# One queue of transfers moved from SyncE to ScalarE, one mean folded into weights, and a new order on five engines

## What is computed

```python
x = x + _L0_conv_ref(_gn(x), ...)      # masked relu, then a 3x3 convolution
x = x + _L1_conv_ref(_gn(x), ...)      # layer norm and a recurrent layer over 784 tokens

def step(carry, inp):                  # one chunk of 16 tokens, 8 heads of 16 channels
    W1c, b1c = carry
    xq, xk, xv, et = inp
    Z1 = xk @ W1c + b1c
    grad = _ln_l2_bwd(Z1, xv - xk, g, bb)
    Attn1 = jnp.tril(xq @ xk.swapaxes(-1, -2))
    b1_bar = b1c - jnp.tril(et) @ grad
    Z1_bar = xq @ W1c - et * Attn1 @ grad + b1_bar
    last_eta = et[..., -1, :, None]
    W1n = W1c - (last_eta * xk).swapaxes(-1, -2) @ grad
    b1n = b1c - (last_eta * grad).sum(-2, keepdims=True)
    return ((W1n, b1n), xq + _ln(Z1_bar, g, bb, EPS_IN))
...
return _ln(out, post_w, post_b, EPS_IN) @ o_w.T
```

## Time and profile before

| what | value |
|---|---|
| three runs | 2008.76, 2009.25, 2012.17 us |
| profiled execution, its span | 2010.2 us |
| PE busy over the span | 1569.5 us (78%) |
| DVE busy | 1582.3 us (79%) |
| POOL busy | 1317.2 us (66%) |
| ACT busy | 977.5 us (49%) |
| first store of the scan to the last | 576.7 to 2005.4 us |

### The profile page before, as it was taken

One profiled execution on the slowest core, in us unless ns is written; L12 is line 12 of the kernel. 1 busy time (PEld: TensorE's weight loads), 2 busy tenths in 40 slices (PEclk: granted clock), 3 DMA queues, 4 the chain that ended last, 5 costly groups with the idle time before them and its releaser, 6 DMA issues.

```text
span 2010.2 us, 82699 instructions
## 1 busy us (share of the span) xinstructions
PE 1569.5 (78%) x33518; PEld 1214.9 (60%) x33518; DVE 1582.3 (79%) x3818; ACT 977.5 (49%) x2358; POOL 1317.2 (66%) x1479
## 2 busy tenths in 40 slices
PE   1886978914678887888788888878887888888886
PEld 1443544502567676677676766766776766767664
DVE  6989998706687877788878878887888788788774
ACT  2223545443455555555555545555555555555452
POOL 1244535465677777777767777777777777677763
PEclk9998989965666667666656666666666666666655
DMA  6058697962555655556656556666565566566553
GB/s 235 1 30 44 98 98 68 77 159 45 65 70 66 76 71 68 73 67 77 74 65 77 70 69 74 72 71 73 67 77 73 67 77 73 65 76 73 69 68 44
DMA packets 1656796, 148.89 MB, mean 74 GB/s; under 512 B 1636448, under 2 KB 1650016, under 8 KB 1656416
## 3 DMA queue, kind: packets, MB, share of 16 engines
q1 hardware_dynamic: 1396912, 117.90, 49.9%
q10 hardware_dynamic: 259504, 25.70, 10.1%
HBM read 40.71 MB, written 38.54 MB: 39 GB/s over the span
## 4 chain that ended last, share of the span: by engine, by line
SPq 54%; PE 17%; DVE 12%; DMA 7%; issue 6%; POOL 3%; ACT 2%; POOLq 0%; DVEq 0%; ACTq 0%
SPq L486 25%; SPq L519 13%; SPq L479 12%; DMA late<-work 3%; PE p_m L1678 3%; PE p_x L1693 3%; DMA xs_scratch<-work 2%; SPq L438 2%; PE p_j L1557 2%; DVE work L1007 2%; SPq L440 1%; DVE work L1033 1%; PE p_y L1736 1%; PE p_y L1693 1%; PE p_out L1752 1%
## 5 line engine op out<-in xcount | busy, mean ns | idle before, releaser
L1648 PE MATMUL p_kt<-fold,kqk 128*128 128x16 f16 x6272 | 199.4, 174 | 166.9 <-DMA kqk<-work 162.8
L1648 PEld LDWEIGHTS p_kt<-fold,kqk 128*128 128x128 f16 x6272 | 190.6, 104 | 197.9 <-issue 161.3
L808 ACT ACTIVATE work<-p_kt 128x512 f16<-128x512 f32 x196 | 146.9, 750 | 317.8 <-PE p_kt L1648 317.8
L1557 PE MATMUL p_j<-work 128*128 128x392 f16 x864 | 158.5, 345 | 22.2 <-DVE work L1131 20.7
L578 POOL TENSOR_TENSOR work<-work,row 128x256 f32<-128x256 f32 x98 | 96.9, 988 | 113.2 <-DVE work L1437 113.2
L1316 DVE TENSOR_TENSOR work<-work 128x256 f16<-128x256 f32 x196 | 155.2, 842 | 15.4 <-ACT work L795 15.4
L1621 PE MATMUL p_j<-wa,work 128*128 128x512 f16 x196 | 119.4, 609 | 58.4 <-DMA work<-xs_scratch_tail 30.0
L590 POOL TENSOR_TENSOR w<-wst,w 128x256 f16<-128x256 f32 x98 | 75.5, 770 | 127.8 <-ACT w L855 127.8
L1693 PEld LDWEIGHTS p_x<-w,late 128*128 128x128 f16 x4704 | 149.5, 106 | 12.0
L634 POOL TENSOR_TENSOR work<-work,rope_s 128x256 f32<-128x256 f32 x196 | 141.0, 740 | 20.0 <-DVE work L1283 20.0
L645 POOL TENSOR_TENSOR work<-work 128x512 f32<-128x512 f32 x98 | 130.8, 1335 | 30.4 <-DVE work L1307 30.1
(11 more groups left out here) (171 smaller groups left out, 4474.3 us busy)
## 6 DMA issues: line engine op xcount, KB each, us to landing
late<-work SPq DMA_DIRECT2D x1176, 32.0 KB, 2.7
kqk<-work SPq DMA_DIRECT2D x392, 64.0 KB, 4.2
out_y<-work ACTq DMA_DIRECT2D x49, 256.0 KB, 6.4
x_scratch<-late SPq DMA_DIRECT2D x24, 392.0 KB, 11.7
xs_scratch<-work SPq DMA_DIRECT2D x24, 392.0 KB, 6.7
work<-x_scratch ACTq DMA_DIRECT2D x49, 192.0 KB, 3.4
work<-xs_scratch SPq DMA_DIRECT2D x48, 192.0 KB, 3.4
late<-in_x SPq DMA_DIRECT2D x8, 784.0 KB, 9.0
```

What stands on the lines that cost most here:

```text
L808: return act.activation(kqt16[:, o, g:g + GP, :, :, :].rearrange("p g h t a -> p g a (h t)"), p_kt[:, :].rearrange("p (g a n) -> p g a n", ...
L1557: mm = pe.matmul(p_conv[b % 2][h][:, 0:HALF].rearrange("o (i j) -> o i j", j=W), convw16[:, w, t, :], pad[:, b % 2, a, r:r + ROWS, c:c + W ...
L1648: mm = pe.matmul(p_kt[:, at:at + CS], part_of(g + k, h, a), fold16[:, :], start=True, stop=True)
```

## The change

`qt_spread` moves from SyncE's program to ScalarE's, where it stands behind the second `qt_copy` of a chunk. Its eight transfers, their sources, destinations and semaphores stay as they are. `rate_gate` still computes Sigmoid on ScalarE. The mean over channels is taken out of the output weights once (`wo_p` minus its mean over the input channels), so the post norm no longer subtracts the mean: `post_shift` goes, and `post_norm` only scales. That costs one more matmul in `fold_tables` and one more subtraction in `fold_weights`. The order inside `turn` is new on all five engines. Most offsets change by whole turns too; PE runs 53 turns instead of 54, SyncE 51 instead of 53.

```diff
+        def turned_parts(c, o):
+            part = kqt16[:, o, :, :, :, :].rearrange("p g h t a -> p (g h) (t a)")
+            return part, ktqt[c % 2][:, o, :, :, :, :, :].rearrange("p g h b t a -> p (g h) b (t a)")
...
             def turn(k):
-                m_spread(k - 4)
-                kt_spread(k - 3)
-                qt_spread(k - 3)
-                kq_spread(k - 2)
                 xs_next(k)
+                kt_spread(k - 2)
+                kq_spread(k - 1)
+                m_spread(k - 2)
...
             @guard_chunk
+            def qt_spread(c):
+                act.wait_ge(qt_copy_done.sem, qt_copy_done.count(2 * c + 1))
+                if c < 2:
+                    act.wait_ge(s_kt_zero[c], 1)
+                else:
+                    act.wait_ge(o_done.sem, o_done.count(2 * c - 3))
+                part, whole = turned_parts(c, 0)
+                for b in range(GB):
+                    at = slice(b * CS, (b + 1) * CS)
+                    act.dma_start(whole[at, :, b, :], part[at]).then_inc(qt_landed.sem(c), 16)
...
-                act.wait_ge(post_shift_done.sem, post_shift_done.count(s))
+                act.wait_ge(post_inverse_done.sem, post_inverse_done.count(s))
...
-                    last = act.activation(on[:, k * C:(k + 1) * C], oo[:, k * C:(k + 1) * C], ACT.Identity, bias=ostd[:, 2, k:k + 1],
-                                          scale=ostd[:, 1, k:k + 1])
+                    last = act.activation(on[:, k * C:(k + 1) * C], oo[:, k * C:(k + 1) * C], ACT.Copy, scale=ostd[:, 1, k:k + 1])
...
             def turn(k):
+                rate_gate(k - 2)
+                z_square(2 * k - 5)
...
+                folded(dve.tensor_tensor(wo_p[:, :], wo_p[:, :], p_x[1][:, SC:SC + C], ALU.subtract))
...
-            def post_shift(s):
...
-                dve.scalar_tensor_tensor(out=ostd[:, 2, :], in0=omv[:, :, 0], scalar=-1.0, in1=ostd[:, 1, :],
-                                         op0=ALU.mult, op1=ALU.mult).then_inc(post_shift_done.sem, 1)
...
+                pe.matmul(p_x[1][:, SC:SC + C], mean_m, wo_p[:, :], start=True, stop=True).then_inc(s_fold, 1)
```

196 lines of the change are left out of this document (88 added, 108 removed).

## The result

| | before | after |
|---|---|---|
| median on the same chip | 2010.72 us (2008.76 to 2016.13, 6 runs) | 2002.45 us (1999.01 to 2004.82, 6 runs) |
| ratio after/before, 95% interval | | 0.9952 [0.9938, 0.9967] |
| profiled execution's span | 2010.2 us | 1997.1 us |
| one turn, from store to store in the middle of the scan | 30.69 us | 30.59 us |

The change gives half a per cent. Only about 4 us of it come from the turns (44 x 0.1 us); in the profiled executions the first store of the scan also comes 6.3 us earlier, at 570.4 us instead of 576.7. The forecast was 1895 us with a range of 1795 to 1985, so the prediction was wrong: the direction held, the size did not, and the time lies above the range.

The account below looks back on a forecast made before the run. The prediction took SyncE's queue of transfer starts as the bound; afterwards two loops, through the folds and through PE, would give a turn of 28.1 us, 2.6 less over 44 turns: 114 us off, so 1895 us, range 1795 to 1985.

Parts of the forecast that it names:

- What bounds the kernel now: SyncE's queue before the change: it starts transfers all the time, 34 starts at 0.9 us fill a turn of 30.7 us.
- Transfers: SyncE keeps 26 of 34 starts, 23.4 us; the eight moved to ScalarE cost 5.2 us, between 3.4 and 7.06.
- The loop through the folds: From one chunk's last fold through copy, ScalarE's starts, g_high, qk_low and kq_spread to the next chunk's last fold: 28.2 us.
- rival 1: Faster than forecast: PE's work alone bounds, turns of 25.5 to 27 us, 1781 to 1847 us; chance 0.20.
- The loop through PE: PE's steps between folds, 20.9 us, plus 7.0 of folds: 27.9 us, 28.6 in the worst case with the table load.
- The hope of a higher clock: On PE: denser work may hold the higher clock for longer, taking 0.5 to 1 us off its loop.
- The table load's price: In PE's loop: the page's 1.38 us of drain per load would give near 30 us, the trace's rows 28.6.
- Small sizes: DVE 23.6 us and POOL 22.8 stay below the loops; added weight folding at most 1 us; pipeline filling unchanged within 8 us.
- Rival 2: Transfers on the two queues get in each other's way: turns of 29 to 30.5 us, 1935 to 2001 us; chance 0.18.
- Rival 4: Slower: ScalarE held up by its own starts, past 30.7 us a turn from 7.65 us of starts, up to 2067 us; chance 0.06.
- Rival 3: Nothing moves because the transfers themselves set the turn: 30.7 us a turn, 2010 us; chance 0.02.
- What was to show it: Signs if right: stores 28.1 us apart, SyncE waiting at kq_spread, ScalarE's starts 4 to 6 us, folds 7, PE over 0.88.

Follow-up runs that it names:

- e6: The kernel before with only the output weights centred (no post_shift, post_norm only scales): 2016.70 us, ratio 1.0007.
- e10: The changed kernel with seven of turned k's eight transfers on SyncE left out: 1959.72 us, a single run.
- e11: The changed kernel with ScalarE's store and loads exchanged, the store now at the end of the turn: 1989.26 us, ratio 0.9886.
- e1: The changed kernel with only one of turned q's eight transfers started on ScalarE, seven left out: 1939.97 us, a single run.
- e14: The changed kernel with turned q's transfers split four and four between ScalarE and SyncE, Sqrt table loaded behind rate_gate, 64 bytes of tile added: 1896.49 us, ratio 0.9459.
- e15: The changed kernel, eight starts kept on ScalarE, with the Sqrt table loaded behind rate_gate and 64 bytes of tile added: 1956.03 us, ratio 0.9758.

## Why the prediction was wrong

**What bounds the kernel now.** Right. 34 starts filled the turn, and e6 shows it from the other side: with 1.3 us of VectorE's work taken out of the turn the time stays.

**Transfers.** SyncE starts 26 instead of 34, and it waits 6.4 us a turn (251.9 + 11.1 + 4.6 us over 41.8 turns). Right. The price of ScalarE's eight was the first wrong step. I took 5.2 us, halfway between 3.4 and 7.06, with the second load's 0.77 us as the dear side of one start. Measured: 7.86 us, above both bounds. The nearest row was not on ScalarE's queue: it was SyncE's start of the same shape. None takes under 0.585 us in any run, on SyncE or on ScalarE, so 3.4 us was never to be had: eight at 0.59 us and seven gaps of 0.04 are 5.0 us. Of the other 2.9 us, taking `kt_spread` away gives 0.9 (e10) and moving the store that stands 2.7 us ahead gives 0.9 (e11). The two do not add up: both act mainly on the first start, which falls from 1.58 to 0.95 in e10 and to 0.62 in e11. So 1.1 us at the least, and perhaps 2, are not accounted for.

On the page of the Trainium skill, DMA: Bandwidth & Descriptors, section "Issuing engines are not separate DMA queues": it calls the time to start a transfer "usually small relative to the DMA itself", and I had set the starts against the turn instead. Against the transfer they are not small here either: a start of turned k or of the attention takes 0.82 to 0.93 us on average, and the transfer has landed 2.4 us after its start began. Its first half, that transfers interleave on the same 16 engines whoever starts them, agrees with e11, where the store is in flight beside `kq_spread` and the landing comes 4.1 us behind the last start instead of 3.5. That the starts themselves become longer is not in that section; e10 and e11 show it.

**The loop through the folds.** Its links are there, but it is not the way that ends last: about 1 us of its 30.59 is a wait for the table load at the first copy. The pieces that I worked out sum to 28.25:

| term | predicted | after |
|---|---|---|
| copy | 0.85 | 0.80 |
| starts, to g_high | 5.2 | 8.02 |
| g_high, qk_high, qk_low, to SyncE | 3.35 | 2.47 |
| first start of kq_spread to fold | 11.85 | 11.77 |
| folds | 7.0 | 7.53 |

The starts are 2.8 us too low and the folds 0.5; the conversions are 0.9 too high, since `g_high` and `qk_high` overlap (1.13 us instead of 1.45), the two parts of `qk_low` overlap too (1.28 instead of 1.7), and the hand-over to SyncE takes 0.03 instead of 0.2. 2.34 us are left. The forecast used 28.1 for the turn, and 44 turns of 2.49 us are 110 us; it missed by 107.

A term was also missing. I let `g_high` run when the starts end and never asked when `g_rated` is ready. It is ready 5.8 us behind the copy. So starts shorter than 0.72 us each would have brought nothing more, and rival 1, down to 1781 us, had no room: with one start left the turn is 29.5 us (e1). The forecast's 28.2 could not be reached by the change as it stands, even at 5.2 us of starts: 30.59 less 1.1 is 29.5.

**The loop through PE.** This is the one that binds, over the starts and PE's own work, and it was the second wrong step. I summed it as if PE never waited between the folds of two chunks: 20.9 us from the end of the last fold to the end of the second `project`. It takes 22.9 us from the start of the last copy, which is about when that fold ends. 1.2 us of the difference is PE's wait ahead of `grad`; the rest fits PE's own steps, which take 0.9 us a turn longer (below). PE waits there since `grad` needs `g_low`, `g_low` needs `g_high`, and `g_high` stands behind the starts. So the starts were in both loops, and I had them in one. I had the table load ahead of the first copy as a worst case of 0.7 to 0.8 us and left it out of the sum. It is real in every turn: the first copy is 1.06 us late, and the early load gives back 0.93 to 0.95 us (e14, e15). PE busy is 1111.04/1289.1 = 0.86, short of the 0.88 named. The hope of a higher clock failed as well: the granted clock is 0.58 against 0.62 in the earlier trace rows, nearer to the lower of its two levels, 1.2 GHz, and PE's work grew from 25.5 to 26.4 us a turn.

**The table load's price.** The Trainium skill's page ScalarE: Activation LUTs, section "What ACT_TABLE_LOAD costs", adds drain to each load; its 1.38 us of drain is not in these traces. The load ends at 1208.80 and the square root starts at 1208.81, and taking a load off the loop is worth under 1 us, less than the load itself.

**Small sizes.** In the kernel before, where SyncE's queue binds, the centred weights cost nothing and gave nothing (e6). No run takes them out of the changed kernel. That filling the pipeline stays the same within 8 us held: it is the 6.3 us of the first store.

**Rivals.** Rival 2 (the transfers get in each other's way) came nearest, with its mechanism and just past its upper end of 2001 us; my 0.18 for it was too low. Rival 4's place is right too, and its threshold of 7.65 us for the eight starts was passed, but the rest of the loop came out shorter than the 23.05 it reckoned with: at 7.86 us the turn is 0.1 us below the old one. Rival 3 came within 8 us of the time by the wrong reason: the DMA engines' share is 0.62, and SyncE waits. Rival 1 fell.

**What was to show it.** Stores 30.6 us apart instead of 28.1; folds of 7.5 us instead of 7; SyncE's wait at `kq_spread` came, though the profile puts most of it down to `grad` (L478), which ends within 0.15 us of `qk_low`; eight starts over 7.6 us, which I had named as the sign of rival 4; `g_high` right behind them.

## To carry to other kernels

Price a moved transfer by the start of the same shape wherever it runs, and add what the change puts beside and ahead of it: here eight starts cost 5.0 us at the shortest and 7.9 in place. Where several loops share the moved step, put it into each of them, and look at the step where they meet to see which comes last: pieces of a loop add up to the turn whether it binds or not. Before counting a gain behind a moved step, look up when the other input of the step behind it is ready, since that caps the gain whatever the step costs. Then split such a group between two queues so that each part fits into a wait that is there anyway (1936 us against 2002), take table loads out of the path, and keep tiles at a multiple of the transfers' piece (64 bytes here; other pieces were not tried).
